# A fused two-layer transformer kernel: the preparation of the weights becomes the head of each engine's own program, its loads in another order, with the first two sequences normalized inside it

## The reference

```python
def _L0_cond_ref(x, cond, ...):
    h = film(rmsnorm(x, norm1_w), cond, film1_w, film1_b)
    Q = h @ q_w + q_b
    K = h @ k_w + k_b
    V = h @ v_w + v_b
    scores = jnp.einsum('bnd,bmd->bnm', Q, K) * D ** (-0.5)
    attn = jax.nn.softmax(scores, axis=-1)
    out = jnp.einsum('bnm,bmd->bnd', attn, V)
    x = x_in + (out @ proj_w + proj_b)
    ...   # then an MLP with norm2_w, film2_w, film2_b
```

## Time and profile before

| | |
|---|---|
| time, median of 3 runs | 1674.11 us (1672.1 to 1675.33) |
| time of the profiled execution | 1675.45 us |
| its span in the trace | 1673.5 us |
| TensorE busy | 1612.1 us, 96% of the span |
| VectorE busy | 1274.2 us, 76% |
| ScalarE busy | 867.6 us, 52% |
| GpSimd busy | 481.6 us, 29% |

### The profile page before, as it was taken

How to read it: one execution, slowest core, us unless ns; L and a number is a source line. 1 busy time by engine, 2 the same in 40 slices (tenths; PEclk the granted TensorE clock), 3 DMA queues, 4 the chain that set the end, 5 groups by cost and what they waited for, 6 DMA issues and landing times.

```text
span 1673.5 us, 42799 instructions
## 1 busy us (share of the span) xinstructions
PE 1612.1 (96%) x14686; PEld 1447.6 (86%) x14686; DVE 1274.2 (76%) x2829; ACT 867.6 (52%) x1759; POOL 481.6 (29%) x636
## 2 busy tenths in 40 slices
PE   6999998999999999899999999999998999999998
PEld 6999998999999999677777777777766999999998
DVE  3798887666666676788888888888884777777775
ACT  1576664333333344677777777767775333333332
POOL 1233331132212132233334343434334222121211
PEclk8999999999999999899999999999999999999999
DMA  6600001000000001233233333333330111111111
GB/s 182 187 21 19 22 19 53 3 3 1 0 0 0 0 1 39 92 104 108 96 102 107 101 100 101 104 104 101 96 107 35 58 39 47 42 42 46 38 50 38
DMA packets 99565, 100.67 MB, mean 60 GB/s; under 512 B 13776, under 2 KB 90000, under 8 KB 99488
## 3 DMA queue, kind: packets, MB, share of 16 engines
q1 hardware_dynamic: 96880, 99.53, 19.1%
q10 hardware_dynamic: 2448, 0.08, 0.1%
q0 software_dynamic: 160, 0.04, 0.1%
HBM read 38.62 MB, written 8.55 MB: 28 GB/s over the span
## 4 chain that ended last, share of the span: by engine, by line
PE 71%; DVE 15%; issue 8%; ACT 1%; DMA 1%; SPq 1%; DVEq 1%; POOL 1%; ACTq 0%; POOLq 0%
PE bank L207 57%; DVE C_negmax L1625 8%; PE bank L1442 5%; PE bank L329 3%; PE bank L1456 2%; DVE C_tmp L1661 1%; DVE a_h_lo L348 1%; PE bank L1491 1%; PE bank L1499 1%; DMA xres<-in_x 1%; DVE C_ytok L1651 1%; DVE C_msplit L1633 1%; SPq L384 1%; DVE B_g_lo L929 1%; PE bank L672 1%
## 5 line engine op out<-in xcount | busy, mean ns | idle before, releaser
L1625 DVE TENSOR_REDUCE C_negmax<-bank 128x4 f32<-128x1024 f32 x256 | 313.4, 1224 | 71.5 <-PE bank L1442 71.0
L1563 ACT ACTIVATE C_probs<-bank 128x1024 f32<-128x1024 f32 x256 | 262.4, 1025 | 119.5 <-PE bank L1456 116.8
L918 ACT ACTIVATE B_g<-bank,B_bias 128x256 f32<-128x256 f32 x256 | 107.5, 472 | 217.0 <-PE bank L207 211.3
L918 ACT ACTIVATE D_g<-bank,D_bias 128x256 f32<-128x256 f32 x256 | 107.5, 471 | 214.6 <-PE bank L207 214.6
L296 POOL TENSOR_TENSOR m_rstd<-m_var,neghalf 128x2 f32<-128x2 f32 x64 | 49.8, 778 | 583.7 <-DVE m_var L287 303.3
L1442 PEld LDWEIGHTS bank<-C_kx,C_qs 64*128 64x128 f32 x1024 | 77.8, 187 | 111.9 <-DVE C_negmax L1625 80.2
L1442 PE MATMUL bank<-C_kx,C_qs 64*128 64x256 f32 x1024 | 130.3, 333 | 26.6 <-DVE C_negmax L1625 15.4
L207 PE MATMUL bank<-B_wt_w_hi,B_g_lo 128*128 128x256 f32 x512 | 146.3, 286 | 5.7 <-DVE B_g_lo L929 5.4
L207 PE MATMUL bank<-D_wt_w_hi,D_g_lo 128*128 128x256 f32 x512 | 146.6, 286 | 2.2 <-DVE D_g_lo L929 1.4
L207 PE MATMUL bank<-m_h_hi,B_wt_w_lo 128*128 128x256 f32 x512 | 146.9, 287 | 0.0
L207 PE MATMUL bank<-m_h_hi,D_wt_w_lo 128*128 128x256 f32 x512 | 146.9, 287 | 0.0
(11 more groups left out here) (251 smaller groups left out, 5053.3 us busy)
## 6 DMA issues: line engine op xcount, KB each, us to landing
C_qs<-C_q_hi SPq DMA_DIRECT2D x128, 128.0 KB
C_kx<-C_k_hi SPq DMA_DIRECT2D x128, 128.0 KB, 2.1
C_qs<-C_q_lo SPq DMA_DIRECT2D x64, 128.0 KB
C_kx<-C_k_lo SPq DMA_DIRECT2D x64, 128.0 KB, 2.1
C_gbc<-mod_rows SPq DMA_DIRECT2D x32, 256.0 KB, 3.4
D_gbc<-mod_rows SPq DMA_DIRECT2D x32, 256.0 KB, 3.3
out<-xres SPq DMA_DIRECT2D x32, 256.0 KB, 3.5
xres<-in_x SPq DMA_DIRECT2D x4, 1792.0 KB, 16.4
```

Of the source, the lines that this page charges most:

```text
L918: ins = eng.activation(g[u][:, d * S:(d + 1) * S], hbank[u][:, d * S:(d + 1) * S], func, bias=per_seq(bias1, 2 * u + d, b))
L1563: e_exp.by(eng.activation(probs[t % NP][:, :], stpair[:, :], ACT.Exp, scale=scl))
L1625: e_max.by(eng.tensor_reduce(m4[:, :, :, j], spair[:, :].rearrange("p (e q k) -> p e q k", e=2, q=TH), AX, ALU.max, negate=True))
```

## The change

The block and its barrier go. What it did becomes `start_tensor`, `start_vector`, `start_scalar`, `start_gpsimd` and `start_sync`, called first in each engine's program of phase A, and the tiles that it needed live on the right of SBUF under the raw MLP weights or with phase A's own. The order inside is new: `w_q` and `w_k` are loaded first, then `w_film1`, then the first sequence of x by itself, then `w_v` and `w_p`. Statistics, root and `xhat` of sequences 0 and 1, and transposes and both parts of sequence 0, are done in it (`STARTED`). The pipeline leaves them out. SyncE issues all of x, `w_film2`, `w_ada`, and also the biases and gate rows that ScalarE issued before, ahead of the store of `orow`. film2, ada0, ada1, gates, the modulation sums and mlp shift move to later iterations, and the loads of the MLP weights wait for `res` of sequence 0.

```diff
+                def start_sync(eng):
...
+                    eng.dma_start(cond[:, :], a["cond_1024"]).then_inc(s_cond, 16)
+                    load(w_q, a["L0_cond_q_w"], s_qk)
+                    load(w_k, a["L0_cond_k_w"], s_qk)
+                    load(w_film1, a["L0_cond_film1_w"], s_f1)
+                    load_x(eng, 0, 1, x_in[0][0])
+                    load(w_v, a["L0_cond_v_w"], s_vp)
+                    load(w_p, a["L0_cond_proj_w"], s_vp)
+                    load_x(eng, 1, X_FIRST - 1, x_in[1][0])
+                    n = (NB - X_FIRST) // X_REST
+                    for c in range(X_REST):
+                        load_x(eng, X_FIRST + c * n, n, x_in[2][0])
+                    load(w_film2, a["L0_cond_film2_w"], s_f2)
+                    load(w_ada, a["L1_cond_w_ada"], s_ada)
+                    with nc.allow_non_contiguous_dma(reason="bias vectors, one element per partition"):
+                        for t, v in ((b_film2, a["L0_cond_film2_b"]), (b_ada, a["L1_cond_b_ada"]),
+                                     (n2, a["L0_cond_norm2_w"])):
+                            eng.dma_start(t[:, :], v.rearrange("(t p) -> p t", p=P)).then_inc(s_late, 16)
+                    for g, lo in enumerate((2 * D, 5 * D)):
+                        eng.dma_start(b_gate[:, g * D:(g + 1) * D],
+                                      a["L1_cond_b_ada"][lo:lo + D].partition_broadcast(NB)).then_inc(s_late, 16)
+                    eng.wait_ge(s_orow, 2)
+                    eng.dma_start(mod_dram[2, :, 0:D], orow[:, :]).then_inc(s_orow, 16)
+                    eng.wait_ge(s_orow, 2 + 16)
...
-                LATE_PE = {"film2": 2, "ada0": 22.5, "ada1": 40, "gates": 59, "mlp shift": 16 * 6 + 9}
-                LATE_DVE = {"modulation": 56, "gate sums": 16 * 4 + 8, "mlp bias": 16 * 7 + 8} | {
+                LATE_PE = {"film2": 54, "ada0": 70, "ada1": 86, "gates": 16 * 5 + 14, "mlp shift": 16 * 6 + 15}
+                LATE_DVE = {"modulation": 16 * 5 + 8, "gate sums": 16 * 6 + 8, "mlp bias": 16 * 7 + 8} | {
...
-                LATE_SP = {"ada": 0, "late loads": 48}
+                LATE_SP = {"late loads": 64}
...
+                STARTED = [(n, 0) for n in ("stats", "root", "xhat", "T", "hi_h", "lo_h")] + [
+                    (n, 1) for n in ("stats", "root", "xhat")]
...
                     def late_loads(b):
-                        n = (NB - X_FIRST) // X_REST
-                        for c in range(X_REST):
-                            load_x(eng, X_FIRST + c * n, n, x_in[1][0])
+                        e_res.wait(eng, FIRST)
                         for w in mlp.w:
                             w.load(eng)
                         mlp.load_biases(eng)
```

More of the change, by code:

```diff
@@ L271, in stats @@
                 if x_in is not None:
-                    s, dmas = x_in[0 if b.reg is None and b.off < X_FIRST else 1]
+                    s, dmas = x_in[2 if b.reg is not None or b.off >= X_FIRST else 1 if b.off else 0]
                     eng.wait_ge(s, 16 * dmas)
@@ new lines, in phase_l0_attention @@
+                s_b, s_mm, s_vp, s_vT, s_vpm, s_cp, s_orow = (sem(n) for n in ("b", "mm", "vp", "vT", "vpm", "cp", "orow"))
+                s_kT, s_lows = sem("kT"), sem("lows")
+                s_qk, s_m, s_bq = (sem(n) for n in ("qk", "m", "bq"))
+                w_q, w_k, w_v, w_p = (start.w[n] for n in "qkvp")
+                w_qT, w_kT, w_vT = (start.wT[n] for n in "qkv")
+                esig, biasj, biaso = start.esig, start.biasj, start.biaso
+                p_x, pT, pm, psh, pf1, pc, pqT, pkT = banks
@@ new lines, in start_gpsimd @@
+                def start_gpsimd(eng):
+                    eng.memset(neghalf[:, :], -0.5)
+                    eng.memset(ident[:, :], 0.0).then_inc(s_id, 1)
+                    eng.wait_ge(s_id, 1)
+                    eng.affine_select(out=ident[:, :], in_=ident[:, :], compare_op=ALU.not_equal, fill=1.0,
+                                      base=0, pattern=[[-1, P]], channel_multiplier=1).then_inc(s_id, 1)
+                    with nc.allow_non_contiguous_dma(reason="bias vectors, one element per partition"):
+                        for t, v, s in [(b_film1, a["L0_cond_film1_b"], s_b1), (n1, a["L0_cond_norm1_w"], s_b1)] + [
+                                (t, a[f"L0_cond_{k}_b"], s_b) for t, k in zip(bcol, "qv")]:
+                            eng.dma_start(t[:, :], v.rearrange("(t p) -> p t", p=P)).then_inc(s, 16)
+                    eng.dma_start(orow[:, :], a["L0_cond_proj_b"].partition_broadcast(NB)).then_inc(s_b, 16)
+                    norm.root(eng, FIRST)
+                    norm.root(eng, SECOND)
@@ L1782, in build @@
             mlp0.w.append(Weight(sb_near, sem_near, "w2", a["L0_cond_mlp_w2"]))
+            with ExitStack() as early:
+                start = Start(on_the_right(early, "Ap_")[0])
             with ExitStack() as raws:
```

294 lines of the change are left out of this document (138 added, 156 removed).

## The result

The changed kernel is slightly slower: 1676.05 us median of 20 runs (1673.42 to 1681.06) against 1672.12 of 20 runs of the kernel before (1665.81 to 1675.33), a ratio of 1.0026 with an interval of 1.0018 to 1.0035. The time forecast, 1674.9, is 1.2 us too low, and the range held it; the likeliest case, no change, did not come about. The difference is 3.9 us where the sum had 0.7.

What follows compares the result with a forecast made beforehand. TensorE, busy 96% of the span, bounds the kernel; only its start can come earlier. S2 5.3 us earlier, minus 3.8 (ada1, gates) and 2.2 (half clock): 0.7 slower, 1676.2; less 1.3 for the median, 1674.9 us. Range 1667.5 to 1679.8.

Steps and rivals of the forecast that it cites:

- the likeliest case, no change: Whole kernel: the earlier start is given back in full, 1674.9 us, own range 1671.0 to 1677.4; chance 0.41.
- the baseline that the sum was made against: Start of the third sequence's scores, S2, at 60.16 us in one profiled execution of 1675.45 us; median 1.3 lower.
- q0 at 26.5: End of preparation: the first query product starts at 26.5 us against 37.87, after 18.8 us of work and 2.3 of waits.
- v2 ends at 43.6: TensorE from q0 to the end of v2: 16.0 us of work plus 1.1 us of waiting before S0.
- The row at 45.2: Row of orow behind 12.2 MB on SyncE's queue: w_ada there at 37, bias elements 3 us, row there at 45.2.
- The slow rival: SyncE's queue: 2,304 single bias elements take 7 us, row there at 49.2, 4.0 us more, 1678.9 us; chance 0.28.
- pT1 at 49.4 after 5.8 us idle: TensorE waits for the row through xb0, root, xhat3 and sequence 1's exponential, 4.2 us with gaps; idle from 43.6.
- The clock behind the gap: TensorE at 1.2 GHz after the idle stretch: pT1 and T3 1.9 us, ada0 3.62, S2 starts at 54.9.
- After the mark: Behind S2's start: ada1 and gates still ahead, 3.8 us, and half clock in the first wide matmuls, 2.2 us.
- In steady phase A no change: Sign to look for: phase A's steady part, where TensorE alone is the chain of waits, stays as it was.
- The clock did not hold: Rival, TensorE keeping its upper clock over the gap before pT1: 4.9 us better than the sum, taken as 1668.9; chance 0.23.
- The row was waited for: Rival, no wait for orow's row before pT1: S2 at 46.3, 10.1 us gained, 1664.0 us; chance 0.08.

Runs made afterwards that it cites:

- the second comparison of the changed kernel: The changed kernel run again, unchanged, beside the kernel before: 1677.33 us (6 runs) against 1671.49, ratio 1.0034.
- the last edit: Changed kernel with root before xb, w_film2 loaded earlier, mlp shift back, orow's store and first-row reads through ScalarE: 1668.91 us, ratio 0.9977; repeated, 1669.61, ratio 0.9973.

## Why the prediction came out as it did

**The step that failed: the baseline that the sum was made against.** The change was set against one execution's S2 at 60.16, and its 1675.45 us were taken to be 1.3 us above the median of three runs; against the 1672.12 of 20 runs they are 3.3 above. Over the four profiles the mean S2 of before is 57.3, not 60.16, and the mean of the last v is 246.9; the changed kernel's three stand at 250.4, 3.5 us later. That is most of the 3.9 and 5.8 us between the medians. The start of before varies by 6.2 us with TensorE's pace and, in one execution, a late w_k. The changed kernel's last v varies by 1.5 us only in three profiles: its pT1 and S2 hang on 12 MB in a queue, and xb0 starts within 0.8 us though q0 varies by 2.5. So where before was quick, the change had nothing to give. Subtracting 1.3 us from the sum was wrong in kind too: the lateness of that execution lay in the part that the change replaces. Without it the forecast would have been 1676.2, against 1676.05 measured. That this is so close is luck in part: the terms below err by up to 3.5 us and cancel.

**q0 at 26.5: 24.61, 1.9 earlier than forecast.** The work started at 4.79, not 5.4, had 1.64 us of waits, not 2.3, and took some 18.2 us, not 18.8. Both products of 8 rows ran at the slow pace that the sum assumed (3.76 and 3.65 us).

**v2 ends at 43.6: 47.1, 3.5 later.** Two waits (1.20 and 1.64 us) stand where I had 1.1: 1.7 more. film2 waited for w_film2 and ran 2.74 us, not 1.86: 0.9 more. From 37.3 to 44.1 TensorE was at 1.2 GHz (29 matmuls in 6 us): some 2.7 us for the wide work behind film2. With the 1.9 from q0 this makes 3.4. The clock fell 12 us ahead of the place where I looked for it.

**The row at 45.2: xb0 at 45.83, right to 0.6, by two errors that cancel.** w_ada landed at 40.5 and not at 37, since the queue moved 292 GB/s in the first 26.8 us, for longer than I had allowed. Behind w_ada there were 0.8 us to the issue of the store (at 41.31), which is SyncE's time for the two gate rows, and the store then took 1.6 us as against 1.5 without elements ahead of it; the 3 us for the elements did not appear. Moving all the small loads behind the store gave 1.3 to 2.1 us. The slow rival needed 5.6 us for them and was wrong.

**pT1 at 49.4 after 5.8 us idle: 49.81 after 2.75.** The chain took 4.0 us against 4.2. The idle time is short only because v2 ended late. It is the row that fixes pT1, whatever TensorE lost before it.

**The clock behind the gap: right, but later.** pT1 and T3 still ran at the upper level, 0.93 us for both where the sum had 1.9. TensorE ran at 1.2 GHz from 50.9 to 57.8 (granted clock 0.51), ada0 took 3.27 us, S2 came at 53.83 (forecast 54.9; the difference is mostly these two).

**After the mark: 6.0 us forecast, 6.5 measured.** S2 was 6.3 us earlier than before's, the last v 0.2 later. The terms are ada1 and gates (3.6 as they ran), the lower clock to 57.8 (some 2), and TensorE's idle time behind the mark, 2.3 us against 0.8, of which 1.66 at 84.82. On the other side stands what the prediction left out: in the kernel before the clock also fell right behind mlp shift, with TensorE busy throughout, and cost some 1.7 us (this row is of the kernel before), while the changed kernel kept 1.00 there (80 to 90 above):

```profile
79.00:83.00 4.00, 4.00 (x24) 4.00 (x23) 2.52 (x10) 0.00 (x0) 0.00 (x0) 0.57 0.00 0
```

These terms come to 5.4 us; 1.1 us of the 6.5 stay unexplained. "In steady phase A no change" held: from 100 us to the last v TensorE is never idle in either kernel.

**The rivals.** The clock did not hold. The row was waited for, and taking that wait away gives 6.4 us by the medians (4.2 in the last v of the profiles). "Slower" came about, but not by its mechanism.

**What stays open.** From the last v to the end of the span the executions took 1421.3 to 1427.9 us: 1422.1 to 1423.3 in the four of before, 1422.0, 1427.6 and 1426.0 in the three of the changed kernel. Part is the clock at the start of phase C. The changed kernel's first and second execution there:

```profile
660.00:700.00 40.00, 32.84 (x282) 25.33 (x280) 29.42 (x51) 21.95 (x34) 8.54 (x14) 0.87 0.21 70
```

```profile
660.00:700.00 40.00, 33.67 (x246) 27.11 (x245) 26.97 (x47) 19.50 (x32) 7.14 (x12) 0.74 0.18 59
```

0.13 of 40 us is 5.2 us of the full clock. The third execution reads 0.74 too; the four of before read 0.83 to 0.87. Nor is it the changed kernel alone: of its three executions and the seven of the edits, seven took more than 1424 us for this part, and none of the four of before did. So a second loss of some 2.5 us in the mean (1425.1 against 1422.6) seems to lie behind phase A, which the account above doesn't have. It would fit with the second comparison of the changed kernel, 5.8 us, and with the last edit, which is 6.5 to 7.4 us ahead at the last v but only 3.5 to 4.3 by the medians. It isn't always at phase C: in the last edit's first profile the granted clock is 0.94 in 240 to 300, where the first two of before have 0.97 and 1.00. What brings it about, no run shows, and the count of profiles is small.

## What to carry to other kernels

Before the first transfer of a result is put behind bulk loads in one queue, add up the bytes ahead of it and look at which engine takes it in order, and what stands behind that instruction; here one position on GpSimd was worth 6.4 us, all that the changed kernel had lost, and another engine's queue 6.1. When a change replaces a stretch, learn how much that stretch varies between executions before summing against one of them: the part that is replaced takes its luck, good or bad, with it. A gain in a start has to be followed through every later wait, since a wait that is removed can uncover another (here pT1's for the row hid S2's for the residual, 5.19 us when all else was mended).

## What the runs showed of the hardware that was not expected

- The issue of a small load of single elements held SyncE for 8.10 us (7.57 to 8.64 in the seven other executions with the same loads in the same place) while 1.5 MB of w_ada and two more such loads stood ahead of it. Those elements did not hold up the store behind them by more than 0.1 us (1.6 us to landing, against 1.5 in the kernel before). With the three loads issued after w_ada had landed, the same issue took 1.56 us (store and rows ahead of the biases).
- The clock fell to 1.2 GHz during film2, about 1 us after its start, behind 1.64 us of waiting (changed kernel, 37.3); in its other two profiles, behind 2.69 and 2.08 us of waiting, all of film2 ran at the lower level (3.50 and 3.47 us). It fell at the end of film2 and ada0 close together with no idle time at all (50.7, granted clock 0.51), and right behind mlp shift in the kernel before (0.57 in 79 to 83). Over the 6 us from 38 on in the changed kernel TensorE did about half the matmuls (29 against 55).
- The same program ended its preparation between 20.7 and 26.9 us in four executions, as the issue of w_ada shows. The granted clock reads 1.00 in 4 to 20 us of all of them, and yet the same product of 8 rows took 3.76 us in one and 1.97 in another: in this stretch the durations tell the pace, and the granted clock does not.
